# Rows of maxima for groups 8 to 15: issued by SyncE between a batch's output store and its loads, instead of by GpSimd

## The chip, the cores and the metric

The kernel runs on one core of a Trainium2 chip. The metric is the device time of one execution in microseconds (us). A core has five engines with their own instruction streams, which wait for one another by semaphores: TensorE (PE in the profile, its weight loads PEld), VectorE (DVE), ScalarE (ACT), GpSimd (POOL) and SyncE (SP), which here issues DMAs only. An engine runs its instructions in the order written. A wait stops all that stands behind it on the same engine.

## The reference

A transformer block on x of shape 8 x 256 x 128 (8 batches, 256 tokens, 128 channels; float32), 16 heads of 8 channels:

```python
x = x + _attention(_adaln(x, c, ...), attention_mask, qkv_w, proj_w, proj_b)
x = x + _mlp(_adaln(x, c, ...), mlp_w1, mlp_b1, mlp_w2, mlp_b2)

# _adaln:     h = x / max(rms(x), eps) * norm_w;  h * scale + shift   (scale, shift from silu(c))
# _attention: attn = q k^T / sqrt(8), masked keys to -inf; p = softmax(attn); (p v) @ proj_w.T + proj_b
# _mlp:       h = x @ w1.T + b1; x1, x2 = split(h); (silu(x1) * x2) @ w2.T + b2
```

The softmax subtracts each query's largest score over the keys. That maximum is what the change is about.

## The kernel before

**Layout.** Channels lie on the partitions, tokens on the free axis. The 8 batches form 4 chunks of 512 tokens (`NC = 4`, two batches per chunk). For the scores, each head's q and k are split in three bf16 parts and stacked along the partitions in `q_stack` and `k_stack` (two heads per unit, 64 rows each). Two rows of each head in `q_stack` (`ROW_MAX`) hold the negated maximum of each query in two bf16 parts, so that the matmul that makes the scores subtracts the maximum as well.

**Units and positions.** There are 64 units (`UNITS`: 8 batches x 8 head pairs). TensorE's loop has positions p = 0 to 71. At position p it makes `query_scores(p)` (L629), from which VectorE takes the maxima (`neg_max`, L1152, two reductions per unit), and `key_scores(p - 8)` (L695), the transposed scores with the maximum subtracted, which ScalarE turns into `p_exp` (L1003, two exponentials per unit). `p_times_v` (L716) follows two units later and gathers a batch's outputs in one bank.

**Groups of maxima.** Four units form a group, k = 0 to 15 (`HALVES`). For each group:

1. GpSimd splits the maxima in two bf16 parts (`max_parts`, L486, L488).
2. TensorE transposes them (`turn_maxima(k)`, L650) at position 4k + 4.
3. For k of 2 and up, ScalarE copies the result to `max_rows[:, k % 2]` (`turned(k)`, L952) after the exponentials of unit 4k - 4. This raises `s_turned`.
4. GpSimd waits for `s_turned` (L491) and issues two DMAs of 4 KB (L496) from `max_rows` to the rows in `q_stack`. They raise `s_mr[k % 2]`.
5. TensorE waits for that semaphore before `key_scores(4k)` (L685), and ScalarE before it overwrites the buffer two groups later (L951).

Behind these DMAs GpSimd's loop has, for some k, work on the first two chunks: `over_sum(c)` (L449), `square_2(c)` (L453, at k = 8 for c = 0 and at k = 12 for c = 1), `parts_h2(c)` (L457, L459), and for k = 6 to 11 pieces of the MLP weights' split (L522, L525). The product of `square_2(c)` is averaged by TensorE (`mean_square_2`, L669).

**Outputs of a batch.** When batch b's `p_times_v` is complete, `drain_output(b)` copies the bank to `o_sb` (L947 on ScalarE; VectorE's L1166 for the last two). SyncE's loop over the batches then calls `store_outputs(b)` (L375: to the DRAM tensor `o_rows`) and `load_outputs(b)`, which waits until the store has landed (L379) and reads the data back in another layout: the denominators to `o_den` (L382) and the numerators to `o_num` (L385). Once both batches of chunk c are loaded, ScalarE takes the logarithm of the denominators (`ln_sum(c)`: L956 waits for both tensors of both batches, L855 is the instruction) after the exponentials of unit 16(c + 1) + 7, and `inverse_sum(c)` (L859) follows one unit later. Then `over_sum(c)` divides, and `project(c)` (L660) multiplies with the projection weights. Chunk 0 takes batches 0 and 1, chunk 1 batches 2 and 3, chunk 2 batches 4 and 5.

The order on each engine is written out by these loops and by the constants at the top of the file. No scheduler moves anything.

Of the kernel before, what the change touches and what calls it, by code (L numbers as in the profile page):

```python
# [15 lines left out]
B, N = 8, 256  # L16
# [3 lines left out]
G = H // 2  # L20
CH = 512
NC = TOK // CH
BC = CH // N
# [17 lines left out]
HEAD_ROWS = D * PITCH  # L41
ROW_MASK = 55
ROW_MAX = 62
STACK_DMAS = 2 * SLOTS + BC
FIRST_DMAS = SLOTS + 1
STACKS = 3
HALVES = 2 * B
# [21 lines left out]
    P_SECOND_PART = (7, 8, 9, 11, 12, 14, 14, 15, 17, 19, 22)  # L69
RING = 3  # L70
RING_TURNS = 2
LAG = 2


# [18 lines left out]
def turn_position(k):  # L93
    return 4 * k + 4
# [10 lines left out]
def ring_items():  # L105
    items = []
    for p in range(UNITS + LEAD):
        if p < UNITS:
            items += [("scores", p, 0), ("scores", p, 1)]
        items += [("turn", k) for k in range(RING_TURNS) if turn_position(k) == p]  # L110
        items += [("project", c) for c in range(NC - 1) if project_position(c) == p]
# [48 lines left out]
def build(nc, x_t, small, mask, front_w, back_w, out_t):  # L160
# [4 lines left out]
    with ctx:  # L165
# [3 lines left out]
        def sem(name):  # L169
            return ctx.enter_context(nc.semaphore(name))  # L170
# [39 lines left out]
        max_rows = sb("max_rows", [2 * G, 2, N], BF16)  # L210
# [21 lines left out]
        with ExitStack() as stacks:  # L232
            k_stack = stacks.enter_context(nc.sbuf_tensor("k_stack", [C, STACKS, G, CH], BF16))
            q_stack = stacks.enter_context(nc.sbuf_tensor("q_stack", [C, STACKS, G, CH], BF16))
# [45 lines left out]
        s_turned = sem("s_turned")  # L280
        s_squares = sem("s_squares")
        s_mp = sem("s_mp")
        s_mr = [sem(f"s_mr{i}") for i in range(2)]
        s_b = sem("s_b")
        s_e = sem("s_e")
        s_pv = sem("s_pv")
# [33 lines left out]
        @block.sync  # L320
        def _(sp):

            def load_x(e):
                t = slice(PIECES[e][0] * N, batches_until(e) * N)
                sp.dma_start(x_sb[:, t], x_t[:, t]).then_inc(s_x[e], 16)

            load_x(0)
            sp.dma_start(small_sb[:, :], small).then_inc(s_in, 16)
            sp.dma_start(mask_sb[:, :], mask).then_inc(s_in_mask, 16)
            sp.dma_start(front[:, :], front_w).then_inc(s_wa, 16)  # L330
            load_x(1)
            for e in range(2, NP):
                load_x(e)
            sp.dma_start(back[:, :], back_w).then_inc(s_wb, 16)

            def ones_rows(i):
                sp.wait_ge(s_fill_q[i], 1)
                sp.dma_start(q_stack[ROW_MASK:C:HEAD_ROWS, i, :, :],
                             ones_row[:, :].unsqueeze(1).to_broadcast([1, 2 * G, CH])).then_inc(s_ones[i], 16)

            def mask_rows(b):
                c, at = b // BC, b % BC * N
                sp.dma_start(k_stack[ROW_MASK:C:HEAD_ROWS, c % STACKS, :, at:at + N],
                             mask_add[b:b + 1, :].unsqueeze(1).to_broadcast([1, 2 * G, N])).then_inc(s_stack[piece_of(b)], 16)

            def part_rows(e, j, stack, side, slots):
                c, at = piece_columns(e)
                for slot in range(SLOTS):
                    if slots[slot] == j:
                        sp.dma_start(stack[slot:C:PITCH, c % STACKS, :, at],  # L350
                                     parts[:, PART_BUFFERS[e], side, j, at]).then_inc(s_stack[e], 16)

            def first_stacks(b):
                for j in range(3):
                    sp.wait_ge((s_part0, s_split, s_last)[j][0], b + 1)
                    part_rows(b, j, q_stack, 0, Q_PARTS)

            def stacks_of(e, j):
                if j == 0:
                    c = PIECES[e][0] // BC  # L360
                    if c >= STACKS:
                        sp.wait_ge(s_b, 2 * BC * G * (c - STACKS + 1))
                    else:
                        ones_rows(c)
                        sp.wait_ge(s_fill_k[c], 1)
                    for i in range(BC):
                        mask_rows(BC * c + i)
                sp.wait_ge((s_part0, s_split, s_last)[j][0], e + 1)
                part_rows(e, j, q_stack, 0, Q_PARTS)
                sp.wait_ge(*((s_part0[1], batches_until(e)), (s_split[1], e + 1), (s_last[1], e + 1))[j])  # L370
                part_rows(e, j, k_stack, 1, K_PARTS)

            def store_outputs(b):
                sp.wait_ge(s_od, b + 1)
                sp.dma_start(o_rows[b].rearrange("q j r t -> (j r) q t"),  # L375
                             o_sb[:, b % 2, :].rearrange("r (q t) -> r q t", q=2)).then_inc(s_ow[b % 2], 16)

            def load_outputs(b):
                sp.wait_ge(s_ow[b % 2], 16 * (b // 2 + 1))  # L379
                c, at = divmod(b, BC)  # L380
                rows = o_rows[b].rearrange("q j (s r) t -> (q j s) r t", s=2)
                sp.dma_start(o_den[:, c, at * N:(at + 1) * N],  # L382
                             rows[:, D:D + 1, :].to_broadcast([H, D, N])).then_inc(
                                 s_or[c] if c < NC - 1 else s_last_den[at], 16)
                sp.dma_start(o_num[:, c, at * N:(at + 1) * N], rows[:, 0:D, :]).then_inc(s_or[c], 16)  # L385

            sp.wait_ge(s_const, 7)
            ones_rows(0)
            sp.wait_ge(s_fill_k[0], 1)
            sp.wait_ge(s_mask, 5)  # L390
            for b in range(BC):
                mask_rows(b)
            for b in range(BC):
                first_stacks(b)
            for e in (2, 3):
                for j in range(3):
                    stacks_of(e, j)
            for b in range(B):
                if b == BC - 1:
                    stacks_of(NP - 1, 0)  # L400
                store_outputs(b)
                load_outputs(b)
                if b == BC - 1:
                    stacks_of(NP - 1, 1)
                    stacks_of(NP - 1, 2)
            for b in range(B):
                c, at = b // BC, (b % BC) * N
                sp.wait_ge(s_out, b + 1)
                sp.dma_start(out_t[:, b * N:(b + 1) * N], out_sb[:, c, at:at + N]).then_inc(s_store, 16)
            sp.wait_ge(s_store, 16 * B)  # L410
# [3 lines left out]
        def _(pool):  # L414
# [64 lines left out]
            for k in range(HALVES):  # L479

                pool.wait_ge(s_ad, drained(item("scores", 4 * k + 3, 1)))
                if k >= 2:
                    pool.wait_ge(*((s_a, item("turn", k - 2) + 1) if k - 2 < RING_TURNS else
                                   (s_turn, k - 2 - RING_TURNS + 1)))
                neg = neg_max[:, k % 2, :, :, :]
# [5 lines left out]
                pool.wait_ge(*((s_ad, drained(item("turn", k))) if k < RING_TURNS else (s_turned, k - RING_TURNS + 1)))  # L491
                c, at = divmod(k // 2, BC)
                q0 = 4 * (k % 2)
                for r in range(2):
                    first = r * HEAD_ROWS + ROW_MAX
                    pool.dma_start(q_stack[first:first + 2, c % STACKS, q0:q0 + 4, at * N:(at + 1) * N],  # L496
                                   max_rows[G * r:G * (r + 1), k % 2, :]).then_inc(s_mr[k % 2], 16)
# [17 lines left out]
                if 6 <= k < 12:  # L515
                    i, second = divmod(k - 6, 2)
# [19 lines left out]
        def _(pe):  # L536
# [142 lines left out]
            def key_scores(u):  # L679
                b, g = divmod(u, G)  # L680
                c, at = b // BC, (b % BC) * N
                v = 2 * u
                if u % 4 == 0:
                    k = u // 4
                    pe.wait_ge(s_mr[k % 2], 32 * (k // 2 + 1))  # L685
                if u == 0:
                    pe.wait_ge(s_inv, 2 * NP)
                if u == 1:
                    pe.wait_ge(s_v_out, NC)
                if v + 1 >= RING:  # L690
                    pe.wait_ge(s_e, v + 1 - RING + 1)
                for t in range(KT):
                    for r in range(2):
                        rows = slice(r * HEAD_ROWS, (r + 1) * HEAD_ROWS)
                        mm = nc.tensor.matmul(bank[:, RING + (v + r) % RING, t * N:(t + 1) * N],  # L695
                                              k_stack[rows, c % STACKS, g, at + t * 128:at + (t + 1) * 128],
                                              q_stack[rows, c % STACKS, g, at:at + N], start=True, stop=True,
                                              tile_position=(r * HEAD_ROWS, 0))
                        if t == KT - 1:
                            mm.then_inc(s_b, 1)  # L700
# [141 lines left out]
        def _(act):  # L842
# [105 lines left out]

            def turned(k):
                act.wait_ge(s_turn, k - RING_TURNS + 1)  # L950
                act.wait_ge(s_mr[k % 2], 32 * (k // 2))  # L951
                nc.scalar.activation(max_rows[:, k % 2, :], bank[0:2 * G, turn_bank(k), 0:2 * 64].bitcast(BF16),  # L952
                                     ACT.Copy).then_inc(s_turned, 1)

# [384 lines left out]
```

## Time and profile before

| | |
|---|---|
| Time, median of 3 runs | 176.41 us (174.44, 176.41, 176.95) |
| Profiled execution's own time | 174.46 us |
| Its span, first to last instruction | 172.7 us |
| Granted TensorE clock, mean | 0.990 |
| Busy over the span: PE / DVE / ACT / POOL | 147.5 / 141.6 / 130.1 / 86.6 us |
| The 32 DMA issues of L496 on POOL | 17.8 us busy, 556 ns each |

The span is that of the profiled execution. The 1.76 us between it and the execution's own time lie around it. Busy time of an engine says how much work it has, not that the end waits for it. The chain of waits says which instruction released which. The attention stage fills about 18 to 131 us of the span, and the MLP follows.

### The profile page before, as it was taken

Reading aid. Unit: us, or ns where it says so; the run is one execution under the profiler, and the core shown is the slowest. Engines: PE = TensorE matmul, PEld = TensorE weight load, DVE = VectorE, ACT = ScalarE, POOL = GpSimd, SP = SyncE. Lnnn points to the kernel's source line nnn. Section 1 sums busy time; section 2 is a strip of 40 time slices with the busy share of each in tenths; the row PEclk is TensorE's granted clock in tenths of the full one; section 3 lists DMA queues with packets and bytes.
Section 4 is the critical chain, followed back from the end, with each engine's and each line's share of the span. In section 5 each row is a group of like instructions: output and inputs, shape, how many; then the busy total and the mean of one; then the engine's idle time right before and its main releaser. Section 6 shows DMA issues by size and latency. Waiting matters only on the chain.

```text
span 172.7 us, 3688 instructions
## 1 busy us (share of the span) xinstructions
PE 147.5 (85%) x1312; PEld 75.4 (44%) x1312; DVE 141.6 (82%) x236; ACT 130.1 (75%) x247; POOL 86.6 (50%) x137
## 2 busy tenths in 40 slices
PE   7679686579979999898979898898799998998992
PEld 7565233323323433343333342332125875785870
DVE  8747896878969999976999886995553999968992
ACT  8379962376969899976999976999779674697640
POOL 8309967967761334456338743326200384525560
PEclk9879999999999999999999999999999999999999
DMA  4836551617401263622022021021120210010103
GB/s 103 265 160 198 170 140 54 182 38 209 135 3 66 67 197 119 179 67 63 1 67 63 6 75 49 8 87 40 63 61 0 78 47 2 0 61 0 61 4 122
DMA packets 15336, 14.28 MB, mean 83 GB/s; under 512 B 2718, under 2 KB 14422, under 8 KB 15318
## 3 DMA queue, kind: packets, MB, share of 16 engines
q1 hardware_dynamic: 13910, 13.12, 24.9%
q0 software_dynamic: 1408, 0.93, 2.0%
q8 instruction: 11, 0.18, 0.4%
q14 instruction: 7, 0.06, 0.1%
HBM read 4.34 MB, written 3.15 MB: 43 GB/s over the span
## 4 chain that ended last, share of the span: by engine, by line
PE 44%; DVE 16%; ACT 15%; issue 13%; POOL 10%; DVEq 0%; ACTq 0%; POOLq 0%
ACT p_exp L1003 11%; PE bank L716 10%; PE bank L629 8%; DVE neg_max L1152 6%; POOL gated_lo L532 5%; PE bank L695 5%; PE bank L564 2%; PE bank L669 2%; PE bank L660 2%; PE bank L601 2%; POOL q_stack L496 2%; PE bank L587 2%; PE bank L766 2%; PE bank L552 1%; DVE rest L1127 1%
## 5 line engine op out<-in xcount | busy, mean ns | idle before, releaser
L1152 DVE TENSOR_REDUCE neg_max<-bank 128x2 f32<-128x512 f32 x128 | 81.7, 687 | 8.4 <-PE bank L629 7.6
L1003 ACT ACTIVATE p_exp<-bank 128x512 f32<-128x512 f32 x128 | 69.2, 594 | 10.0 <-PE bank L695 8.9
L716 PE MATMUL bank<-p_exp,v_all 128*25 128x256 f32 x512 | 40.3, 388 | 0.6
L629 PE MATMUL bank<-k_stack,q_stack 62*128 62x256 bf16 x256 | 25.2, 272 | 9.3 <-DVE neg_max L1152 7.3
L532 POOL TENSOR_TENSOR gated_lo<-rs,gated_hi 128x512 fp32r<-128x512 f32 x14 | 18.4, 1311 | 26.4 <-ACT gated_hi L1032 25.2
L496 POOL DMA_DIRECT2D q_stack<-max_rows x32 | 17.8, 556 | 26.1 <-ACT max_rows L952 22.7
L695 PE MATMUL bank<-q_stack,k_stack 64*128 64x256 bf16 x256 | 25.1, 270 | 4.2 <-ACT p_exp L1003 4.2
L629 PEld LDWEIGHTS bank<-k_stack,q_stack 62*128 62x128 bf16 x256 | 8.4, 94 | 34.4 <-DVE neg_max L1152 28.7
L695 PEld LDWEIGHTS bank<-q_stack,k_stack 64*128 64x128 bf16 x256 | 11.0, 94 | 12.5 <-ACT p_exp L1003 7.6
L716 PEld LDWEIGHTS bank<-p_exp,v_all 128*25 128x25 f32 x512 | 9.4, 102 | 15.7 <-ACT p_exp L1003 8.2
L766 PE MATMUL bank<-h_hi,w_parts 128*128 128x512 f32 x32 | 13.1, 409 | 0.5 <-DVE rs L1285 0.3
L1032 ACT ACTIVATE gated_hi<-rs 128x512 fp32r<-128x512 f32 x14 | 8.8, 630 | 6.1 <-DVE rs L1285 6.1
L1277 DVE SCALAR_TENSOR_TENSOR xn<-bank,small_sb,h 128x512 f32<-128x512 f32 x16 | 11.9, 743 | 1.1 <-ACT h L1039 1.1
L486 POOL CAST max_parts<-neg_max 128x16 bf16<-128x16 f32 x16 | 3.1, 195 | 18.8 <-DVE neg_max L1152 18.8
L767 PE MATMUL bank<-h_lo,w_parts 128*128 128x512 f32 x32 | 12.5, 391 | 0.0
L768 PE MATMUL bank<-h_hi,w_parts 128*128 128x512 f32 x32 | 12.5, 391 | 0.0
L1285 DVE SCALAR_TENSOR_TENSOR rs<-bank,small_sb,xn 128x512 f32<-128x512 f32 x16 | 12.0, 751 | 0.6
L1039 ACT ACTIVATE h<-bank,small_sb 128x512 f32<-128x512 f32 x16 | 10.9, 679 | 1.5 <-PE bank L768 1.5
L466 POOL DMA_DIRECT2D k_stack<-parts x12 | 6.4, 541 | 6.6 <-ACT parts L893 6.6
L438 POOL TENSOR_TENSOR parts<-rest,parts 128x512 bf16<-128x512 f32 (+1 forms) x8 | 8.1, 1033 | 0.0
L766 PEld LDWEIGHTS bank<-h_hi,w_parts 128*128 128x128 f32 x32 | 6.0, 188 | 4.0 <-issue 1.8
L552 PE MATMUL bank<-mean_w 128*128 128x128 f32 x28 | 6.1, 404 | 1.0 <-POOL mean_w L415 1.0
(117 smaller groups left out, 218.7 us busy)
## 6 DMA issues: line engine op xcount, KB each, us to landing
q_stack<-parts SPq DMA_DIRECT2D x18, 128.0 KB
k_stack<-parts SPq DMA_DIRECT2D x18, 128.0 KB
o_rows<-o_sb SPq DMA_DIRECT2D x8, 256.0 KB, 2.1
o_den<-o_rows SPq DMA_DIRECT2D x8, 128.0 KB, 3.2
o_num<-o_rows SPq DMA_DIRECT2D x8, 128.0 KB, 3.1
out_t<-o_num SPq DMA_DIRECT2D x8, 128.0 KB, 1.9
back<-back_w SPq DMA_DIRECT2D x1, 832.0 KB, 7.9
x_sb<-x_t SPq DMA_DIRECT2D x3, 256.0 KB, 5.2
```

Source lines behind the costliest of these rows:

```text
L496: pool.dma_start(q_stack[first:first + 2, c % STACKS, q0:q0 + 4, at * N:(at + 1) * N], max_rows[G * r:G * (r + 1), k % 2, :]).then_inc(s_m ...
L532: nc.gpsimd.tensor_tensor(gated_lo[:, n % GB, :], gated[:, n % GB, :], gated_hi[:, n % GB, :].bitcast(F32), ALU.subtract).then_inc(s_gated ...
L629: mm = nc.tensor.matmul(scores[r][:, t * N:(t + 1) * N], q_stack[rows, c % STACKS, g, at + t * 128:at + (t + 1) * 128], k_stack[rows, c % ...
L695: mm = nc.tensor.matmul(bank[:, RING + (v + r) % RING, t * N:(t + 1) * N], k_stack[rows, c % STACKS, g, at + t * 128:at + (t + 1) * 128], ...
L716: mm = nc.tensor.matmul(bank[32 * j:32 * j + V_WINDOW, 6 + b % 2, half * N:(half + 1) * N], v_all[:, b, t, :, :].rearrange("p h w -> p (h ...
L766: nc.tensor.matmul(out, w_hi, h2_hi[:, c, :], start=True, stop=False)
L767: nc.tensor.matmul(out, w_hi, h2_lo[:, c, :], start=False, stop=False)
L768: nc.tensor.matmul(out, w_lo, h2_hi[:, c, :], start=False, stop=True).then_inc(s_w1, 1)
L1003: nc.scalar.activation(p_exp[:, u % 4, par, :, :], bank[:, RING + v % RING, :].rearrange("p (t q) -> p t q", t=KT), ACT.Exp, scale=D ** -0 ...
L1152: nc.vector.tensor_reduce(out=neg_max[:, k % 2, :, par, g], in_=bank[:, n % RING, :].rearrange("p (t k) -> p t k", t=KT), axis=AX.X, op=AL ...
L1277: nc.vector.scalar_tensor_tensor(out=silu[:, n % 2, :], in0=bank[:, first, :], scalar=vec[:, V_B1 + m:V_B1 + m + 1], in1=sig_x1[:, n % 2, ...
L1285: nc.vector.scalar_tensor_tensor(out=gated[:, n % GB, :], in0=bank[:, first + 1, :], scalar=b1, in1=silu[:, n % 2, :], op0=ALU.add, op1=AL ...
```

## The change

Groups 0 to 7 stay as they are. For groups 8 to 15 (`ROWS_BY_SP = 8`) the two DMAs are issued by SyncE. They raise a semaphore pair of their own, `s_mr_late`, and the two places that waited for `s_mr` now ask `rows_landed(k)` which pair and which count apply. Within batch b = 2 to 5 SyncE's order becomes: store of b, rows of group 2b + 4, loads of b, rows of group 2b + 5. GpSimd's wait for `s_turned` at L491 stays in the code for every group; only the two DMAs behind it go.

```diff
+ROWS_BY_SP = 8
...
         s_mr = [sem(f"s_mr{i}") for i in range(2)]
+        s_mr_late = [sem(f"s_mr_late{i}") for i in range(2)]
+
+        def rows_landed(k):
+
+            if k < ROWS_BY_SP:
+                return s_mr[k % 2], 32 * (k // 2 + 1)
+            return s_mr_late[k % 2], 32 * ((k - ROWS_BY_SP) // 2 + 1)
...
+            def rows_of_maxima(k):
+                sp.wait_ge(s_turned, k - RING_TURNS + 1)
+                c, at = divmod(k // 2, BC)
+                q0 = 4 * (k % 2)
+                for r in range(2):
+                    first = r * HEAD_ROWS + ROW_MAX
+                    sp.dma_start(q_stack[first:first + 2, c % STACKS, q0:q0 + 4, at * N:(at + 1) * N],
+                                 max_rows[G * r:G * (r + 1), k % 2, :]).then_inc(s_mr_late[k % 2], 16)
+
             for b in range(B):
                 if b == BC - 1:
                     stacks_of(NP - 1, 0)
                 store_outputs(b)
+                if ROWS_BY_SP <= 2 * b + 4 < HALVES:
+                    rows_of_maxima(2 * b + 4)
                 load_outputs(b)
+                if ROWS_BY_SP <= 2 * b + 4 < HALVES:
+                    rows_of_maxima(2 * b + 5)
...
-                for r in range(2):
+                for r in range(2 if k < ROWS_BY_SP else 0):
                     first = r * HEAD_ROWS + ROW_MAX
                     pool.dma_start(q_stack[first:first + 2, c % STACKS, q0:q0 + 4, at * N:(at + 1) * N],
...
-                    pe.wait_ge(s_mr[k % 2], 32 * (k // 2 + 1))
+                    pe.wait_ge(*rows_landed(k))
...
-                act.wait_ge(s_mr[k % 2], 32 * (k // 2))
+                act.wait_ge(*rows_landed(k - 2))
```

On SyncE, in the loop over the batches, one odd batch (b = 3, whose buffer semaphore is `s_ow1`) of the kernel before:

```order
L375 DMA o_rows<-o_sb 128x2x256 [waits s_od]
L382 DMA o_den<-o_rows 128x1x256 [waits s_ow1]
L385 DMA o_num<-o_rows 128x1x256
```

and of the changed one, with groups 10 and 11 around the loads (L384, L391 and L394 are the same three instructions):

```order
L384 DMA o_rows<-o_sb 128x2x256 [waits s_od]
L413 DMA q_stack<-max_rows 2x4x256 [waits s_turned]
L413 DMA q_stack<-max_rows 2x4x256
L391 DMA o_den<-o_rows 128x1x256 [waits s_ow1]
L394 DMA o_num<-o_rows 128x1x256
L413 DMA q_stack<-max_rows 2x4x256 [waits s_turned]
L413 DMA q_stack<-max_rows 2x4x256
```

The loads now stand behind a wait for `s_turned` and two DMAs more.

On GpSimd, in its loop over the groups, group 8 of the kernel before (`square_2(0)` is L453):

```order
L488 TENSOR_TENSOR max_parts<-neg_max,max_parts 128x4x4 [waits s_mp]
L496 DMA q_stack<-max_rows 2x4x256 [waits s_turned]
L496 DMA q_stack<-max_rows 2x4x256
L453 TENSOR_TENSOR sq<-rest 128x512 [waits s_ad]
L525 CAST w_parts<-back 128x512
```

and of the changed one (L510, L475 and L547 are L488, L453 and L525):

```order
L510 TENSOR_TENSOR max_parts<-neg_max,max_parts 128x4x4 [waits s_mp]
L475 TENSOR_TENSOR sq<-rest 128x512 [waits s_ad,s_turned]
L547 CAST w_parts<-back 128x512
```

The square keeps the wait for `s_turned` and loses the two DMAs ahead of it.

## Rows read from the trace of the kernel before

**Rows 1.** The page, chain that ended last: share of the span by engine.

```profile
PE 44%; DVE 16%; ACT 15%; issue 13%; POOL 10%; DVEq 0%; ACTq 0%; POOLq 0%
```

**Rows 2.** Timeline, POOL, group 8: start, us, instruction, idle before it.

```profile
77.92 1.12 POOL L496 DMA_DIRECT2D q_stack<-max_rows  x2 [2.21 <-ACT max_rows L952]
79.06 1.05 POOL L453 TENSOR_TENSOR sq<-rest 128x512 f32<-128x512 f32 x1
```

**Rows 3.** Chain of waits, 76 to 82 us: start, us, what.

```profile
77.39 0.25 ACT max_rows L952
77.64 0.28 issue
...
80.26 1.10 PE bank L669 x2
```

**Rows 4.** Timeline, PE: mean of squares, chunks 0 and 1.

```profile
79.03 0.63 PE L716 MATMUL bank<-p_exp,v_all 128*25 128x256 f32 x8
80.26 1.10 PE L669 MATMUL bank<-sq,mean_w 128*128 128x512 f32 x2 [0.60 <-POOL sq L453]
...
105.03 1.10 PE L669 MATMUL bank<-sq,mean_w 128*128 128x512 f32 x2 [0.60 <-POOL sq L453]
```

**Rows 5.** Waits, 75 to 125 us: who waited for whom, total, times, longest.

```profile
PEld bank L695 <- DMA q_stack<-max_rows: 0.7, 1, 0.7
PE bank L650 <- POOL max_parts L488: 0.5, 1, 0.5
```

**Rows 6.** Chain of waits, 94 to 98 us.

```profile
94.29 0.12 ACT o_den L855
...
96.54 1.05 ACT p_exp L1003 x2
...
97.64 0.63 PE bank L716 x8
```

**Rows 7.** Timeline, SP's queue, batch 3.

```profile
87.47 0.37 SPq L375 DMA_DIRECT2D o_rows<-o_sb  x1
89.56 0.51 SPq L382 DMA_DIRECT2D o_den<-o_rows  x1
90.12 0.94 SPq L385 DMA_DIRECT2D o_num<-o_rows  x1
```

**Rows 8.** Timeline, SP's queue: two small DMAs of mask rows.

```profile
58.12 1.14 SPq L343 DMA_DIRECT2D k_stack<-mask_add  x2
```

**Rows 9.** Timeline, PE's weight loads: first key scores of group 14.

```profile
118.70 0.14 PEld L695 LDWEIGHTS bank<-q_stack,k_stack 64*128 64x128 bf16 x4 [0.73 <-DMA q_stack<-max_rows]
```

**Rows 10.** Timeline, ACT: output of batch 3, copy of group 10, logarithm of chunk 1.

```profile
86.84 0.60 ACT L947 ACTIVATE o_sb<-bank 128x512 f32<-128x512 f32 x1
...
90.57 0.36 ACT L952 ACTIVATE max_rows<-bank 16x256 bf16<-16x256 bf16 x1
...
94.18 0.63 ACT L855 ACTIVATE o_den<-o_den 128x512 f32<-128x512 f32 x1
```

**Rows 11.** L375, L385, L350 over the span: issue ns min/median/max; L385's landing.

```profile
L375 SPq DMA_DIRECT2D o_rows<-o_sb x8: 366/367/406, 53.3 to 134.1; - x8
...
L385 SPq DMA_DIRECT2D o_num<-o_rows x8: 591/604/1382, 56.0 to 136.8; - x8
...
DMA to landing us min/median/max: 2.7/3.1/3.4
...
L350 SPq DMA_DIRECT2D q_stack<-parts x30: 532/598/802, 11.8 to 70.2; - x30
```

**Rows 12.** L385 of batch 3 alone: from issue to landing.

```profile
DMA to landing us min/median/max: 2.9/2.9/2.9
```

**Rows 13.** Timeline, ACT: copy of group 14, logarithm of chunk 2.

```profile
115.35 0.36 ACT L952 ACTIVATE max_rows<-bank 16x256 bf16<-16x256 bf16 x1
...
118.96 0.63 ACT L855 ACTIVATE o_den<-o_den 128x512 f32<-128x512 f32 x1
```

**Rows 14.** L385 of batch 5 alone: from issue to landing.

```profile
DMA to landing us min/median/max: 2.7/2.7/2.7
```

## The prediction

> **What bounds the kernel now.** I read the chain of waits first. No engine holds the end alone: PE has 44% of it, DVE, ACT and POOL 10 to 16% each [rows 1]. So a saving or a stall counts only where the chain passes through it, and the place decides. I then laid the timelines of POOL, PE, ACT and SP's queue side by side over 75 to 125 us, where groups 8 to 15 are handled, and asked at each moved DMA two things: who stands behind it on the queue that it leaves, and who stands behind it on the queue that it joins.
>
> **What POOL gives back.** Each group takes two issues, 1.12 us together [rows 2], so 8 groups free about 9 us of POOL. Most of that is worth nothing, because POOL then waits for the next maxima anyway. The reader is to see two exceptions, groups 8 and 12. There the chain runs from ACT's copy through the two issues to the square and to PE [rows 3]. PE stood idle 0.60 us for the square, in both chunks [rows 4]. In the changed kernel POOL still waits for the copy, so the square cannot begin before 77.64 + 0.28 = 77.92. It ends at 77.92 + 1.05 = 78.97 instead of 80.1. PE's work before it ends at 79.03 + 0.63 = 79.66 [rows 4], so PE itself is late next and only its idle time goes. Of 1.12 us saved PE takes 0.60, less some 0.05 to start, so 0.55. Group 12 shows the same idle time. **Gain: 2 x 0.55 = 1.1 us.**
>
> POOL's earlier split of group 11's maxima would also take away 0.5 us that PE waited at L650 [rows 5]. I cost it at nothing: the chain there lies on ACT, from 94.29 to 97.6 without another engine [rows 6], and if that cover were gone it would give at most 0.5 us.
>
> **The rows themselves.** SP starts closer behind ACT than POOL: the store of batch 3 left at 87.47, 0.03 us after ACT's output copy ended at 86.84 + 0.60 = 87.44, while POOL needed 0.28 us [rows 3, 7, 10]. Its small issues last as long as POOL's, 1.14 us for two against 1.12 [rows 2, 8]. So the rows leave at about the same time, at most 0.3 us earlier. Between 75 and 125 us TensorE waited once for rows, 0.7 us [rows 5], at group 14 [rows 9]. In the changed kernel ACT is late at that place for another reason (the stall of batch 5, below), so I cost the rows' landing at nothing. If they landed 1 us later than from POOL, the first cover to go would be that of groups 10 and 14, and both lie inside the stall of the next part.
>
> **What the loads lose.** They used to go as soon as the store had landed, 2.1 us after it: at 89.56 and 90.12 for batch 3 [rows 7]. Now SP first waits for the copy of group 10, which ACT ends at 90.57 + 0.36 = 90.93 [rows 10], and issues two DMAs. Nobody waits for the loads of batches 2 and 4 soon, since their chunk is complete only with batch 3 or 5. The loads of batches 3 and 5 have a user close behind: ACT's logarithm, three units after the copy. ACT runs it in line, ahead of its exponentials.
>
> Step by step for batch 3. SP starts the rows at 90.96 (0.03 behind the copy). For the cost of the two issues the trace has no row of this shape on SP. The nearest is the mask rows, small DMAs to stack rows: 1.14 us for two [rows 8]. The ends are the store's 0.37 us, 0.82 for two with the gaps, and twice an ordinary 0.67 us (between the 0.60 and 0.80 of L350), 1.42 [rows 11]. I take 1.14. The denominators' issue takes 0.51 with a gap of 0.04 behind it [rows 7] (0.61 together at the high end), so the numerators are issued at 90.96 + 1.14 + 0.55 = 92.65. They land 2.9 us later [rows 12]: 95.55. ACT began the logarithm at 94.18 [rows 10]. Stall: 95.55 - 94.18 = 1.4 us. The time to landing goes from 2.7 to 3.4 over the eight batches [rows 11]. With both low ends the stall is 90.96 + 0.82 + 0.55 + 2.7 - 94.18 = 0.85 us, with both high ends 90.96 + 1.42 + 0.61 + 3.4 - 94.18 = 2.2 us.
>
> Batch 5 the same: the copy ends at 115.71 [rows 13], SP starts at 115.74, the numerators go at 117.43 and land 2.7 us later [rows 14], at 120.13. The logarithm began at 118.96 [rows 13]. Stall 1.2 us, with the same ends.
>
> The Trainium skill (DMA: Bandwidth & Descriptors, section "Anatomy of one DMA — SWDGE (gpsimd) path") gives a DMA about 2.0 us fixed plus its bytes at 436 GB/s, which I apply to SP's loads as an estimate: 2.3 us for 128 KB. By it each stall would be 0.8 us and the sum below about +0.5 us instead of +1.5. The trace speaks against it: none of these loads landed in less than 2.7 us [rows 11].
>
> Does the stall reach the end? Behind the logarithm ACT is on the chain without a pause until PE needs its exponentials at 97.64 [rows 6], and PE's next work waits for them in order. PE can run ahead by no more than the three banks between the scores and the exponentials. So I let it through whole. **Loss: 1.4 + 1.2 = 2.6 us.**
>
> **Sum.** -1.1 + 2.6 = +1.5 us. The profiled execution took 174.46 us (span 172.7), so it would take 176.0. It was one of the fast ones: the median of the runs is 176.41, 1.95 us above it. On the median the forecast is **177.9 us**, or 0.9% more. About 2% is what a measurement of this kernel can tell from no change, 3.5 us here, so this counts as no change, with a lean to slower.
>
> **The rivals.**
>
> *Gain without stall (10%).* The loads land before the logarithm, or their delay is made up in ACT's later pauses. Then -1.1 stands alone: 173.4 on the profiled execution, 175.3 on the median. For it: the chain holds 13% in which an engine waited for nothing that the profile shows [rows 1], and the two tensors land beside each other, so a quieter queue could speed both. Against it: the numerators would have to land 1.2 to 1.4 us sooner than every row says, and behind the logarithm the chain is ACT alone [rows 6].
>
> *Stall without gain (13%).* The square is no earlier for PE, because the wait for the copy that POOL keeps is longer than its last wait shows, or because the time comes back as a wait for VectorE. Then +2.6: 177.1, or 179.0 on the median. For it: POOL's wait stays. Against it: the idle time is put to the square by name [rows 4].
>
> *Slower beyond 2% (12%).* SP's issues are the mechanism. Behind other traffic an issue of L385 took up to 1.38 us, and 0.94 in batch 3 itself [rows 7, 11]. If a row DMA takes that long on SP, the loads leave later by what the two take beyond 1.14 us. It decides where the two stalls reach 3.5 + 1.1 = 4.6 us together, 2.3 each, so 1.0 us more per pair, or 1.07 us per row issue. At 1.38 us each the pair is 1.6 us dearer, and the sum is 2.6 + 3.2 - 1.1 = +4.7: 179.2, or 181.1 on the median. Against it: the small row DMAs on SP took about 0.57 us [rows 8], and the long issues belong to transfers of 128 KB.
>
> *Faster beyond 2% (3%).* No row shows 3.5 us that POOL's issues could give back.
>
> **How the numbers follow.** The forecast has 62%: between its ends, 2 x 0.85 - 1.1 = +0.6 and 2 x 2.2 - 1.1 = +3.3 us, so 177.0 to 179.7 on the median. The range must take in the first two rivals, 175.3 and 179.0. The runs before spread from 174.44 to 176.95, so a median can come out 1 us lower by that alone. I take 174.4 to 179.8, which leaves out the slow rival and the fast one. Faster 0.03; slower 0.12; within 2% the rest, 0.85.
>
> **What would show it.** In the changed profile: (1) PE's idle time at the mean of squares, 0.60 us twice, is gone or below 0.1 us. (2) SP's queue has the rows at about 0.03 us behind ACT's copy, two issues in about 1.1 us, then the loads; those of batches 3 and 5 go about 2.5 us later behind their store than before. (3) ACT's logarithm of chunks 1 and 2 has idle time before it, 1.2 to 1.4 us, put to the loads; chunk 0's has none. (4) Nobody waits longer for the rows than before. (5) The span grows by about 1.5 us. The prediction is wrong if the logarithm does not wait, if the wait is there but the next exponentials make it up, or if SP's row issues differ much from 0.57 us.

## The result and the profile after

The changed kernel took 181.01 us (median of 4 runs, 179.83 to 181.5) against 175.53 us for the kernel before on the same chip (4 runs, 174.44 to 176.95): a ratio of **1.031**, 95% interval 1.025 to 1.037. It is 3% slower. The forecast was 177.9 us, within 174.4 to 179.8, and no change. The slow side had 12%. Ratios and their intervals, here and below, leave out runs more than 1.5% above the fastest of the same kernel.

The page of the changed kernel, its TensorE clock in 40 slices (tenths of full speed) and the chain by engine, answering to [rows 1]. The span is 178.0 us, 5.3 more than before.

```profile
PEclk9999999699999999999999999999579999999999
...
PE 36%; DVE 19%; issue 12%; ACT 12%; DMA 9%; POOL 8%; SPq 3%; DVEq 0%; ACTq 0%; POOLq 0%
```

Two things are new. DMAs and SP's queue stand on the chain, 12% of it together, and the clock dips late, in slices 29 and 30, which are 125 to 133 us. The dip in slice 8 lies in the start of the kernel, which has dips in the kernel before too; the account below comes to it.

The chain of waits of the changed kernel, 91 to 98 us (start, us, what), is the step that the prediction worked out for batch 3:

```profile
91.71 0.24 ACT max_rows L974
91.95 0.02 issue
91.97 0.61 SPq L413
...
92.62 0.61 SPq L413
...
93.27 0.58 SPq L391
...
93.89 2.71 DMA o_num<-o_rows
96.61 0.02 issue
96.63 0.02 ACT o_den L877
```

Copy, two row DMAs, the denominators' issue, the numerators' transfer, logarithm: nothing else lies between. The timeline of ACT shows the two stalls, which answer to [rows 10, 13] (L877 is L855 of before, in brackets the idle time):

```profile
96.63 0.63 ACT L877 ACTIVATE o_den<-o_den 128x512 f32<-128x512 f32 x1 [1.33 <-DMA o_num<-o_rows]
...
122.07 0.63 ACT L877 ACTIVATE o_den<-o_den 128x512 f32<-128x512 f32 x1 [1.28 <-DMA o_num<-o_rows]
```

And the two places where POOL should give time back, which answer to [rows 4], have lost their idle time (PE):

```profile
80.78 1.12 PE L691 MATMUL bank<-sq,mean_w 128*128 128x512 f32 x2
...
106.73 1.12 PE L691 MATMUL bank<-sq,mean_w 128*128 128x512 f32 x2
```

What the sum did not have stands 3 us behind the second stall. PE's timeline there, the first two rows still at full clock:

```profile
123.24 0.39 PE L717 MATMUL bank<-q_stack,k_stack 64*128 64x256 bf16 x4 [1.54 <-ACT p_exp L1025]
123.57 0.63 PE L738 MATMUL bank<-p_exp,v_all 128*25 128x256 f32 x8
124.97 0.61 PE L717 MATMUL bank<-q_stack,k_stack 64*128 64x256 bf16 x4 [0.77 <-ACT p_exp L1025]
125.51 1.07 PE L738 MATMUL bank<-p_exp,v_all 128*25 128x256 f32 x8
126.50 2.08 PE L682 MATMUL bank<-o_num,back 128*128 128x512 f32 x2
```

L717 goes from 0.39 to 0.61 us, L738 from 0.63 to 1.07, and L682 takes 2.08 us, where chunk 1's took 1.12. Busy time of the engines over that stretch (window, its length, busy us and instructions of PE, PEld, DVE, ACT and POOL, then the granted clock as a share of 2.4 GHz, the DMA share and GB/s), first of the changed kernel:

```profile
122.00:124.00 2.00, 0.76 (x12) 0.26 (x12) 0.00 (x0) 1.93 (x5) 0.00 (x0) 1.00 0.03 8
124.00:126.00 2.00, 1.23 (x16) 0.31 (x12) 1.29 (x2) 1.72 (x4) 0.00 (x0) 0.64 0.01 3
126.00:128.00 2.00, 2.00 (x10) 0.50 (x2) 0.00 (x0) 0.76 (x2) 0.00 (x0) 0.50 0.38 132
128.00:130.00 2.00, 2.00 (x13) 0.31 (x12) 1.35 (x2) 0.79 (x2) 0.00 (x0) 0.50 0.17 35
```

and of the kernel before:

```profile
120.00:122.00 2.00, 1.12 (x16) 0.37 (x16) 0.66 (x2) 2.00 (x6) 0.92 (x2) 1.00 0.04 8
122.00:124.00 2.00, 1.92 (x16) 0.52 (x14) 0.63 (x2) 1.34 (x3) 0.18 (x1) 1.00 0.26 86
124.00:126.00 2.00, 1.73 (x24) 0.48 (x24) 1.44 (x2) 1.45 (x3) 0.00 (x0) 1.00 0.14 50
```

PE was busy 0.76 of the 2 us from 122 to 124, idle 1.54 us at a stretch, then its clock went from 2.4 to 1.2 GHz for some 6 us.

**The account.** To see where the 5.3 us arise I took the starts of ScalarE's copies of the maxima, one per group, and of the logarithm for chunk 2's second norm, in the changed kernel and in the one before, and subtracted. The steps of that difference are the terms. The change ran twice (the second profile is that of e7 below).

| up to | before, us | change, first profile | step | change, second profile | step | what lies in the step |
|---|---|---|---|---|---|---|
| group 8 | 77.27 | 78.46 | +1.19 | 77.46 | +0.19 | code that is the same |
| group 9 | 84.44 | 84.99 | -0.64 | 83.99 | -0.64 | square of chunk 0 |
| group 10 | 90.57 | 91.58 | +0.46 | 90.59 | +0.47 | VectorE's normalization of chunk 0 |
| group 11 | 95.74 | 98.12 | +1.37 | 97.27 | +1.51 | first stall |
| group 12 | 102.05 | 104.41 | -0.02 | 105.08 | +1.50 | behind it |
| group 13 | 109.21 | 110.93 | -0.64 | 111.61 | -0.63 | square of chunk 1 |
| group 15 | 120.43 | 123.56 | +1.41 | 124.31 | +1.48 | second stall |
| norm, chunk 2 | 128.63 | 134.02 | +2.26 | 133.85 | +1.34 | behind it, part at half clock |

Behind the norm nothing more than 0.1 us is added. The first row lies in code that the change does not touch. The start's clock differs between profiles: it was 0.91 of full in 0 to 20 us of the kernel before and in 20 to 40 us of the change's first profile. Another 0.37 us of the 1.19 came at group 7, where ScalarE's logarithm of chunk 0 waited 0.28 us for its loads. The second profile of the change has no such wait; e1, e5 and e9 below have one. From group 8 to the norm the change added 4.20 us in one profile and 5.03 us in the other, so it is more than 2% slower without the start too.

### The profile page after: what moved, and what is told of

It is laid out like the page before. It is cut to its first block, busy times and chain, and to the rows that moved or that the text cites. A ratio compares the mean times of both kernels' runs of the same rounds, so it can differ in the third digit from the quotient of the medians.

```text
span 178.0 us, 3695 instructions
## 1 busy us (share of the span) xinstructions
PE 150.9 (85%) x1312; PEld 75.2 (42%) x1312; DVE 142.1 (80%) x236; ACT 130.5 (73%) x247; POOL 77.8 (44%) x121
## 4 chain that ended last, share of the span: by engine, by line
PE 36%; DVE 19%; issue 12%; ACT 12%; DMA 9%; POOL 8%; SPq 3%; DVEq 0%; ACTq 0%; POOLq 0%
PE bank L738 9%; ACT p_exp L1025 8%; DVE neg_max L1174 7%; PE bank L651 6%; POOL gated_lo L554 5%; DMA o_num<-o_rows 5%; PE bank L717 4%; PE bank L682 2%; PE bank L691 2%; DVE rest L1149 2%; PE bank L788 2%; DMA q_stack<-max_rows 2%; PE bank L598 1%; PE bank L623 1%; SPq L413 1%
## 5 line engine op out<-in xcount | busy, mean ns | idle before, releaser
L738 PE MATMUL bank<-p_exp,v_all 128*25 128x256 f32 x512 | 41.6, 399 | 0.5
L717 PE MATMUL bank<-q_stack,k_stack 64*128 64x256 bf16 x256 | 26.0, 279 | 7.5 <-ACT p_exp L1025 7.3
L717 PEld LDWEIGHTS bank<-q_stack,k_stack 64*128 64x128 bf16 x256 | 11.0, 96 | 17.4 <-ACT p_exp L1025 11.2
L738 PEld LDWEIGHTS bank<-p_exp,v_all 128*25 128x25 f32 x512 | 9.5, 103 | 16.2 <-ACT p_exp L1025 8.2
L518 POOL DMA_DIRECT2D q_stack<-max_rows x16 | 8.8, 554 | 14.2 <-ACT max_rows L974 9.3
L488 POOL DMA_DIRECT2D k_stack<-parts x12 | 6.4, 543 | 5.4 <-ACT parts L915 5.4
L598 PE MATMUL bank<-h,front 128*128 128x512 f32 (+1 forms) x10 | 5.6, 651 | 1.2 <-ACT h L896 1.2
```

The costliest lines, as they stand in the source:

```text
L738: mm = nc.tensor.matmul(bank[32 * j:32 * j + V_WINDOW, 6 + b % 2, half * N:(half + 1) * N], v_all[:, b, t, :, :].rearrange("p h w -> p (h ...
```

## The experiments

The theory after this reading: the loads' lateness makes two stalls, each stall leaves PE idle, the clock falls behind it, and the sum of both is the loss. The gain at the squares is as forecast.

The whole time of a run carries the start with it, and the start varies more than most of the effects below. PE's clock in 20 to 40 us, first of the kernel before, then of e3:

```profile
20.00:40.00 20.00, 13.69 (x89) 6.42 (x88) 16.89 (x32) 10.94 (x23) 15.78 (x22) 1.00 0.40 114
20.00:40.00 20.00, 15.70 (x68) 8.05 (x64) 12.57 (x23) 6.18 (x13) 11.87 (x16) 0.66 0.41 113
```

So here is the same account for the profile of every experiment, against the profile of the kernel before: how late it is at group 8, before anything was changed, and what it adds from there to the norm of chunk 2.

| profile | late at group 8, us | added from group 8 to the norm, us |
|---|---|---|
| change, first | +1.19 | +4.20 |
| change, second (e7) | +0.19 | +5.03 |
| e1, rows behind the loads | +0.57 | -0.90 |
| e2, ahead in batch 3 alone | +1.00 | +0.52 |
| e3, ahead in batch 5 alone | +4.33 | +1.04 |
| e4, change with matmuls in the second gap | +2.64 | +2.14 |
| e9, change with matmuls in both gaps | +4.04 | +2.03 |
| e5, late loads only | +1.75 | +4.00 |
| e6, e1 with a wait in group 9 | +2.28 | -1.36 |
| e8, groups 8 and 12 alone | +3.28 | -1.25 |

**e1: both pairs of rows behind the loads of their batch.**

```diff
                 store_outputs(b)
-                if ROWS_BY_SP <= 2 * b + 4 < HALVES:
-                    rows_of_maxima(2 * b + 4)
                 load_outputs(b)
+                if ROWS_BY_SP <= 2 * b + 4 < HALVES:
+                    rows_of_maxima(2 * b + 4)
                 if ROWS_BY_SP <= 2 * b + 4 < HALVES:
                     rows_of_maxima(2 * b + 5)
```

> The change, with both pairs of row DMAs behind the loads of their batch. Theory (the loads stood behind the wait for the copy and two issues, and the logarithm of chunks 1 and 2 stalled for them): no idle time before the logarithm, the clock stays at its upper level over 121 to 134 us, and the two 0.6 us in front of the mean of squares stay saved: 0.993 of the time before, about 1.2 us less. Rival (row DMAs on SyncE's queue are themselves the cost, by landing late or by disturbing other transfers): still 1.5% or more slower than before, with TensorE waiting for the rows.

Measured: 0.989 of the time before (0.976 to 1.002), which cannot be told from no change but is clear of the change's 1.031. Its ACT timeline has the logarithm of chunk 1 without idle time:

```profile
93.60 1.09 ACT L1028 ACTIVATE p_exp<-bank 128x512 f32<-128x512 f32 x2 [0.17 <-PE bank L720]
94.58 0.63 ACT L880 ACTIVATE o_den<-o_den 128x512 f32<-128x512 f32 x1
```

The clock reads 1.00 throughout 40 to 136 us. SyncE still issues all eight groups' rows. So the row DMAs on its queue cost nothing that can be seen. Their place ahead of the loads is what cost.

**e2 and e3: the rows ahead of the loads in one batch alone, 3 or 5.**

```diff
-                if ROWS_BY_SP <= 2 * b + 4 < HALVES:
+                if ROWS_BY_SP <= 2 * b + 4 < HALVES and b in ROWS_FIRST:
                     rows_of_maxima(2 * b + 4)
                 load_outputs(b)
+                if ROWS_BY_SP <= 2 * b + 4 < HALVES and b not in ROWS_FIRST:
+                    rows_of_maxima(2 * b + 4)
```

> The change, with the rows ahead of the loads in batch 3 alone, behind them in the others. Theory: one stall of 1.4 us before the logarithm of chunk 1, none before that of chunk 2, clock up throughout: -1.2 + 1.4 = +0.2 us, a ratio of 1.00. Rival (a stall anywhere lowers the clock): the clock falls too and the ratio is 1.01 or more.

> The change, with the rows ahead of the loads in batch 5 alone. Theory (only the stall of chunk 2, behind the last query scores, leaves TensorE idle enough for its clock to fall): one stall of 1.3 us and the clock at half over some 6 us behind it, 2.2 us more: -1.2 + 1.3 + 2.2 = +2.3 us, a ratio of 1.013. Rival (the fall of the clock in the profiled run was chance, or needs both stalls): +0.1 us, a ratio of 1.00.

Measured: e2 1.0105 (1.004 to 1.017), e3 1.019 (1.006 to 1.032). Each has its one stall in the profile, 1.29 us before the logarithm of chunk 1 in e2, 1.33 us before that of chunk 2 in e3, and none before the other. In e2's profile the clock stays up. In e3's it falls behind the stall:

```profile
122.00:124.00 2.00, 1.25 (x14) 0.41 (x14) 0.40 (x1) 0.67 (x2) 0.42 (x2) 1.00 0.42 120
124.00:126.00 2.00, 1.02 (x12) 0.31 (x12) 0.00 (x0) 2.00 (x5) 0.00 (x0) 0.71 0.03 8
126.00:128.00 2.00, 1.88 (x20) 0.31 (x12) 1.29 (x2) 1.72 (x5) 0.00 (x0) 0.50 0.01 4
```

There it had risen again by about 128 us and cost 0.5 us (8.70 us from group 15's copy to the norm, 8.20 before), not the 2.2 that I had expected. Both ratios came out higher than the theory's 1.00 and 1.013. The account does not bear that out: from group 8 on e2 adds 0.52 us (theory +0.2; 0.47 of it comes at VectorE's normalization, see e6 below) and e3 1.04 us (theory +2.3). The 1.019 of e3 is for the most part the start, +4.33 us in its profile, and all four of its runs have a mean clock (0.952 to 0.962) near that of the profiled one (0.952). So its time does not price the second stall. For e2 two reasons are possible, a late start or the 1.5 us behind the first stall that the second profile of the change has. Ten runs of e2 go from 175.76 to 179.89 us, and only one has a trace, so this stays open.

**e4 and e9: matmuls in PE's gaps.** e4 has five of 128 x 128 in the second stall (the branch `p == UNITS + 1` alone), e9 four more in the first. Their results are overwritten.

```diff
+                if p == 49:
+                    idle_bank = ring_bank(item("scores", 50, 0))
+                    for _ in range(FILLERS - 1):
+                        nc.tensor.matmul(idle_bank[:, 0:C], mean_w[:, :], mean_w[:, :], start=True, stop=True)
+                if p == UNITS + 1:
+                    idle_bank = ring_bank(item("project", NC - 2))
+                    for _ in range(FILLERS):
+                        nc.tensor.matmul(idle_bank[:, 0:C], mean_w[:, :], mean_w[:, :], start=True, stop=True)
```

> The change as it is, with five matmuls of 128 x 128 whose results are overwritten, in TensorE's stream where it stood idle for 1.5 us in the stall of chunk 2. Theory (half of the loss is the clock that falls behind that stall): both stalls before the logarithm stay, the clock stays up, and about 2.2 us of the change's loss come back: a ratio to before of 1.018 instead of 1.031. Rival (the clock's fall costs nothing that the wait for the loads would not cost anyway): 1.031 as before, or more by the fillers.

> e4, with four more such matmuls of 128 x 128 in TensorE's gap of the first stall (chunk 1), whose results are overwritten too. Theory (the first stall lowers the clock in some executions and the second in nearly all, and the fall costs by itself): both waits of the logarithm stay, 1.3 to 1.5 us each, the clock stays up behind both, and what is left of the loss is 2 x 1.4 - 1.2 + 0.5 = +2.1 us: a ratio of 1.012, and less scatter than e4. Rival (the waits for the loads cost the whole 3% and the clock nothing): 1.03, or more by the fillers.

Measured: e4 1.014 (1.001 to 1.027), e9 1.004 (0.998 to 1.010). The median of all 13 runs of e9 is 178.61 us, 1.010 of the 176.77 us of the kernel before beside it. They scatter more than e4's (175.79 to 180.50 us against 177.93 to 180.83), not less as expected, and the profile is of the longest of them. PE's timeline of e4 at the second stall (five matmuls are ten records):

```profile
123.23 1.38 PE L833 MATMUL bank<-mean_w 128*128 128x128 f32 x10
124.88 0.39 PE L718 MATMUL bank<-q_stack,k_stack 64*128 64x256 bf16 x4 [0.27 <-ACT p_exp L1030]
...
127.65 1.13 PE L683 MATMUL bank<-o_num,back 128*128 128x512 f32 x2
```

The projection takes 1.13 us again, not 2.08. From group 15's copy to the norm it is 8.21 us in e4 and 8.20 in e9, as in the kernel before (8.20), against 10.46 and 9.54 in the change. Both waits of the logarithm are still there (1.36 and 1.32 us in e9). More work on PE made the stretch faster, so the clock's fall costs by itself. The account prices it better than the ratio of e4, whose interval is wide: from group 8 to the norm e4 adds 2.14 us and e9 2.03, where the change adds 4.20 and 5.03. That is about half of the change's loss, and e9's theory of +2.1 us. What the four matmuls in the first gap do is not shown: without them the clock fell behind the first stall in one profile (e7) of five, and e9 has one profile.

**e5: late loads without any row DMA on SyncE.** The kernel before, with one wait added:

```diff
                 sp.wait_ge(s_ow[b % 2], 16 * (b // 2 + 1))
+                if b in LATE:
+                    sp.wait_ge(s_e, 2 * (G * b + 13) + 2)
```

> The kernel before, all row DMAs on GpSimd; on SyncE only the loads of batches 3 and 5 wait until ScalarE has done the exponentials of the second unit behind the copy (about when the changed kernel issues them), with no DMA added to the queue. Theory (lateness of the loads is the whole loss): stalls of about 1.2 and 1.0 us before the logarithms and 2 us of clock behind the second: about +4.2 us, a ratio of 1.024. Rival (the row DMAs on SyncE's queue matter by themselves): 1.01 or less.

Measured: 1.033 (1.025 to 1.040), 180.64 us. The wait as written lets the loads go after the first unit behind the copy, not the second, 1.03 us behind the copy in batch 3 where the change needed 1.33. So the stalls are shorter than the change's, 0.90 and 1.00 us, and the clock falls behind the second all the same:

```profile
121.00:124.00 3.00, 1.46 (x20) 0.46 (x18) 0.70 (x2) 2.00 (x5) 1.18 (x3) 1.00 0.30 83
124.00:127.00 3.00, 2.57 (x24) 0.51 (x24) 1.29 (x2) 2.72 (x7) 1.11 (x2) 0.57 0.02 3
127.00:130.00 3.00, 3.00 (x14) 0.81 (x14) 0.67 (x1) 0.54 (x2) 0.00 (x0) 0.50 0.26 91
```

A loss of the change's size is there without its DMAs. From group 8 on it is 4.00 us, 0.94 and 1.14 for the stalls and 1.91 behind the second, against the 4.2 expected. What lifts the ratio above the 1.024 of the theory lies in the profile at the start, +1.75 us.

**e7: the change once more.**

> The changed kernel once more, beside the others of this call. Theory: 1.03 within the interval, clock at half behind the stall of chunk 2 again. Rival (the clock's fall was chance): the clock stays up in this profile and the ratio is 1.015.

Measured: 1.029 (1.022 to 1.036), 180.43 us. The clock fell behind the second stall again, and this time behind the first too, 99 to 103 us:

```profile
99.00:101.00 2.00, 1.92 (x18) 0.61 (x16) 0.76 (x2) 1.67 (x4) 1.78 (x2) 0.55 0.04 12
101.00:103.00 2.00, 2.00 (x12) 0.68 (x10) 1.07 (x2) 1.08 (x2) 0.42 (x2) 0.59 0.38 131
```

**e6 and e8: where the gain lies, and what ate part of it.** e6 is e1 with a wait in group 9: GpSimd's product for the weights' split comes after VectorE's normalization of chunk 0. e8 moves only groups 8 and 12 to SyncE, behind the loads.

```diff
                     if second:
                         pool.wait_ge(s_w_parts, 2 * i + 1)
+                        if k == 9:
+                            pool.wait_ge(s_xn2, 1)
```

```diff
+BY_SP = (8, 12)
...
                 load_outputs(b)
+                if 2 * b + 4 in BY_SP:
+                    rows_of_maxima(2 * b + 4)
```

> e1 (rows behind the loads), and in group 9 GpSimd's product for the MLP weights' split waits until VectorE has done the normalization of chunk 0. Theory (with its DMAs gone GpSimd runs this product 0.9 us earlier, over VectorE's normalization, and the two block each other: 1.14 us instead of 0.68): that instruction is back to 0.68 us, and 0.4 us more is gained than in e1: a ratio of 0.986 to 0.99. Rival (1.14 us has another cause): it stays at 1.14 us and the ratio is e1's.

> Only groups 8 and 12, the two with the square behind them on GpSimd, are issued by SyncE, behind the loads; the other fourteen stay on GpSimd. Theory (the whole gain of the move lies at these two places, 0.6 us each, and without group 9's move the product does not meet VectorE's normalization): about 1.2 us less, a ratio of 0.993 or a little below, with the normalization at 0.68 us. Rival (the relief of GpSimd in the other groups counts): clearly less gain than e1.

Measured: e6 0.990 (0.985 to 0.994), e8 0.992 (0.987 to 0.997). In the changed kernel, as in e1, VectorE's normalization took 1.14 us where it took 0.68 before (DVE, then POOL, of the changed kernel):

```profile
86.10 1.14 DVE L1212 SCALAR_TENSOR_TENSOR o_den<-parts,rest 128x512 f32<-128x512 f32 x1
```

```profile
85.42 1.27 POOL L544 TENSOR_TENSOR w_parts<-back,w_parts 128x512 fp32r<-128x512 f32 x1 [1.31 <-ACT max_rows L974]
```

GpSimd's product runs from 85.42 to 86.69, and the normalization begins inside it. In e6 the two follow each other:

```profile
87.19 0.68 DVE L1217 SCALAR_TENSOR_TENSOR o_den<-parts,rest 128x512 f32<-128x512 f32 x1
```

```profile
88.04 1.27 POOL L549 TENSOR_TENSOR w_parts<-back,w_parts 128x512 fp32r<-128x512 f32 x1 [2.83 <-DVE o_den L1217]
```

By the account from group 8 on, e8 gains 0.64 and 0.63 us and nothing anywhere else, e1 gains the same two and gives 0.47 back at the normalization, and e6 has no such step. The times of the three cannot be told apart by their intervals. The intervals of e6 and e8 exclude 1.000, but the gain of 1% is less than the 2% that counts as a change here.

The Trainium skill (SBUF — State Buffer, section "Who interferes with whom") says that a VectorE instruction with two inputs in SBUF contends with a GpSimd instruction that reads SBUF. The trace agrees: VectorE's took 1.14 us in overlap, 0.68 without. GpSimd's, which had begun first, took 1.27 us both times.

## Why the prediction was wrong

- **The gain at the squares: right.** Forecast 1.1 us for both; 0.64 and 0.63 in both profiles. PE's own work was late next, as said.
- **The rows themselves: right.** SP started 0.03 us behind the copy (91.94, 91.97). In e1 they cost nothing, and in the change TensorE waited for them once, 0.7 us, as before. Two issues took 1.26 us in batch 3, not 1.14, inside the bounds.
- **The loads: right in place and size.** Stalls of 1.33 and 1.28 us on ACT, 1.37 and 1.41 in the account; forecast 1.4 and 1.2. For batch 3 two errors cancel: the numerators were issued 1.95 us behind the copy, not 1.72, and landed in 2.71 us, not 2.9. The 2.3 us by the Trainium skill (DMA: Bandwidth & Descriptors, section "Anatomy of one DMA — SWDGE (gpsimd) path") was an estimate from a fit for DMAs issued by GpSimd; for these loads, issued by SyncE, it is too short. The sign that chunk 0's logarithm has no idle time held in the second profile only: in the first it waited 0.28 us for a load, ahead of anything changed.
- **"Does the stall reach the end?": the step that failed.** I let the stall through whole, and took that for the worst case. The end moved by more than the stall. The sum lacked a term for what PE's clock does behind an idle PE: 2.3 us in the first profile, 1.5 + 1.3 in the second. The kernel could have led me there: at its start it has 14 matmuls that by their name serve nothing else (`keep_clock`, L552), and the clock dips in its profile there all the same. And the second stall lies where the query scores are over, where PE was busy in the kernel before only 1.12 of the 2 us from 120 to 122.
- **"Earlier work on POOL is worth nothing": not quite.** It cost 0.47 us at the normalization. I had asked what POOL's freed time would help, not what its earlier work would collide with.
- **The sum.** -1.3 (squares) + 2.8 (stalls) = +1.5, the number forecast, but by luck to that digit: both terms were 0.2 us larger than forecast and cancel. With 2.2 behind the stalls, 0.5 for the collision and 1.2 at the start, where the change has no part, it is +5.4 at the norm and +5.3 at the end. The ratio of 1.031 is 5.5 us. Without the start the first profile explains 4.1 of it and the second, whose clock fell twice, 4.9.
- **The rivals.** "Slower beyond 2%" came true in the time and not in its mechanism: row issues took 0.61 to 0.72 us, far from the 1.07 where it would decide. The range's upper end was too low because no case held the clock.

What stays open: why the first stall lowers the clock in one profile of the change (e7) and not in the other, nor in those of e2, e4 and e5. Length alone does not decide it: ScalarE waited 1.46 us and PE stood idle 1.40 us in e7, where the clock fell, and 1.48 and 1.42 us in e4, where it stayed up. Nor is it known what sets the clock in the start, which moves whole times by up to 4 us.

## What to carry to other kernels

Before a DMA is put on another queue, look at what stands behind it there and how soon each has its user: here two 0.6 us issues were harmless behind the loads and cost 3% ahead of them. Price a stall that leaves TensorE idle for more than a microsecond not by its length alone, but with the matmuls behind it at half clock, above all where TensorE's load is thin already. Read small effects from the stretch that the edit touches, since the whole time also carries a start that varies by more. When an engine is relieved, its later work moves forward, and may then overlap with work on another engine that it never met before.

## What the runs showed of the hardware

- Waits of 1.0 to 1.3 us on ScalarE at the second stall, with TensorE idle 1.3 to 1.6 us at a stretch, brought TensorE's granted clock from 2.4 to 1.2 GHz for some 3 to 7 us behind them, in all four profiles with that stall and no added matmuls (the change twice, e3, e5). Five matmuls of 128 x 128 in the gap kept it up in both profiles that had them (e4, e9). At the first stall, with idle stretches up to 1.4 us, it fell in one profile of five. The Trainium skill (TensorE: Matmul & The Clock Gate, section "What's actually happening") describes a clock gate set by how busy TensorE has recently been; these profiles agree with that: idle gaps came ahead of the falls, and matmuls in the gap kept it up.
- A row DMA of 4 KB took 0.61 to 0.72 us to issue on SyncE in the changed kernel and 0.56 on GpSimd [rows 2]: here SyncE was not the quicker one to issue it.
- The start of the kernel, the same code in all, ran with 0.66 (e3) to 1.00 (before, e1, e7) of the clock in 20 to 40 us, and the kernel before took 174.4 to 179.2 us in its runs.
